# A different prologue for the attention part of a one-core attention and expert kernel: unit rows set by VectorE, idle transposes, more maxima and values before the main loop

## The reference

```python
x = x + attention(layernorm(x))      # 8 heads, each of two softmaxes over D = 32
#   q, k = x @ Wq, x @ Wkv[:, :512]; v = x @ Wkv[:, 512:]
#   w = softmax(q1 k1^T) - lam * softmax(q2 k2^T); attn = rms_norm(w @ v) * gamma
x = x + experts(layernorm(x))        # gated q, k, v projections of 16 experts,
#   causal attention with head dimension 64, gated output projections
```

## Time and profile before

| quantity | value |
|---|---|
| median of 3 runs | 1513.02 us (1511.97 to 1514.63) |
| the profiled execution | 1515.15 us, span 1513.4 us |
| first chunk of scores starts (span time) | 55.23 us |
| first maximum of the main loop starts on VectorE | 57.62 us |
| last projection of the attention part ends | about 1163.7 us |
| TensorE busy | 1398.9 us (92%) |

### The profile page before, as it was taken

The page is one execution under the profiler, slowest core; times in us unless marked ns, Lnnn a source line. Parts: engine busy times, 40 slices in busy tenths (PEclk is TensorE's granted clock), DMA queues, the critical chain, the costliest instruction groups (busy, mean ns, idle before and its releaser), DMA issues.

```text
span 1513.4 us, 56871 instructions
## 1 busy us (share of the span) xinstructions
PE 1398.9 (92%) x25690; PEld 1107.2 (73%) x25690; DVE 1022.8 (68%) x1379; ACT 854.7 (56%) x1698; POOL 554.5 (37%) x528
## 2 busy tenths in 40 slices
PE   3699999999999999999999999999996179999997
PEld 1367777777777777777777777777775169898986
DVE  5877676666766676667666676766622687888885
ACT  3255565656656555665656555565563346666663
POOL 4322323233342323243232323332232295656550
PEclk9799999999999999999999999999997579999999
DMA  4201011010101011110101011110002233333320
GB/s 117 53 14 34 15 33 25 22 36 12 45 8 39 13 34 24 24 34 13 45 6 41 13 34 24 24 34 13 3 3 44 72 144 121 147 120 129 139 93 11
DMA packets 42177, 70.34 MB, mean 46 GB/s; under 512 B 14800, under 2 KB 25296, under 8 KB 37840
## 3 DMA queue, kind: packets, MB, share of 16 engines
q1 hardware_dynamic: 40848, 65.65, 14.9%
q10 hardware_dynamic: 1088, 1.05, 0.3%
HBM read 38.88 MB, written 2.36 MB: 27 GB/s over the span
## 4 chain that ended last, share of the span: by engine, by line
PE 88%; DVE 6%; issue 2%; ACT 1%; POOL 1%; DMA 1%; ACTq 0%; SPq 0%; DVEq 0%; POOLq 0%
PE att_ps L559 31%; PE st_ps L543 15%; PE ring_ps L610 14%; PE qkv_ps L717 8%; PE ring_ps L597 4%; PE rest_ps L732 3%; DVE part_max L1181 2%; PE t_ps L805 2%; PE ring_ps L590 2%; PE ring_ps L636 2%; PE rest_ps L790 1%; PE ring_ps L628 1%; PE t_ps L757 1%; POOL z L516 1%; PE qk_ps L744 1%
## 5 line engine op out<-in xcount | busy, mean ns | idle before, releaser
L1181 DVE TENSOR_REDUCE part_max<-ring_ps 128x2 f32<-128x1024 f32 x512 | 623.8, 1223 | 328.9 <-PE ring_ps L610 319.7
L559 PEld LDWEIGHTS att_ps<-v_sb,pT 128*64 128x64 f32 x16384 | 632.8, 138 | 145.3 <-issue 28.8
L559 PE MATMUL att_ps<-v_sb,pT 128*64 128x65 f32 x16384 | 650.7, 222 | 2.4 <-issue 2.4
L872 ACT ACTIVATE pT<-st_ps 128x512 f32<-128x512 f32 x1024 | 554.5, 608 | 169.7 <-PE st_ps L543 163.4
L543 PE MATMUL st_ps<-qa,ka 98*64 98x512 f16 x2048 | 398.3, 386 | 4.4 <-issue 3.8
L610 PE MATMUL ring_ps<-ka,qa 96*64 96x512 f16 x2048 | 310.3, 382 | 9.8 <-DVE part_max L1181 5.3
L516 POOL TENSOR_TENSOR z<-xnT,rw_wide 128x512 f32<-128x512 f32 x128 | 169.5, 1331 | 108.4 <-DVE z L1372 93.4
L880 ACT ACTIVATE raw_attn<-att_ps 128x260 f32<-128x260 f32 x128 | 49.6, 388 | 205.7 <-PE att_ps L559 205.7
L543 PEld LDWEIGHTS st_ps<-qa,ka 98*64 98x64 f16 x2048 | 115.4, 110 | 67.0 <-issue 13.5
L717 PE MATMUL qkv_ps<-ew_split,z 128*128 128x192 f16 x1536 | 142.8, 252 | 11.2 <-DVE z L1372 11.2
L717 PEld LDWEIGHTS qkv_ps<-ew_split,z 128*128 128x128 f16 x1536 | 132.0, 100 | 14.5 <-issue 10.8
(11 more groups left out here) (202 smaller groups left out, 1215.1 us busy)
## 6 DMA issues: line engine op xcount, KB each, us to landing
rw_wide<-rows_of_weights SPq DMA_DIRECT2D x32, 1024.0 KB, 5.1
qa<-split SPq DMA_DIRECT2D x192, 64.0 KB, 2.0
ka<-split SPq DMA_DIRECT2D x180, 64.0 KB, 2.0
resid<-in_L_attn_x SPq DMA_DIRECT2D x4, 512.0 KB, 8.0
out<-yo SPq DMA_DIRECT2D x32, 64.0 KB, 1.5
qa<-shift_rows ACTq DMA_DIRECT2D x62, 4.0 KB
ka<-split ACTq DMA_DIRECT2D x12, 64.0 KB, 2.0
wkv_sb<-in_L_attn_Wkv SPq DMA_DIRECT2D x1, 512.0 KB, 6.1
```

What stands on the lines that cost most here:

```text
L559: mm = pe.matmul(att_ps[q0:q0 + TILE_COLS, qt * DV1:(qt + 1) * DV1], pT[:, blk % 2, kt, qt * P + q0:qt * P + q0 + TILE_COLS], v_sb[:, j % ...
L872: act.activation(pT[:, blk % 2, kt, :], st_ps[:, c % ST_BANKS, :], ACT.Exp).then_inc(exp_ok, 1)
L1181: dve.tensor_reduce(part_max[:, which % 2, 2 * quarter + m // 2, m % 2, :], pair.rearrange("p (n k) -> p n k", n=2), AX.X, ALU.max, negate ...
```

## The change

- GpSimd's two memsets of the unit rows go; VectorE does them as its first instructions, with a semaphore `units_set`.
- TensorE makes 28 transposes of the identity matrix (`WARM_UP`), whose result nobody reads, as soon as batch 0 is centred (`ln_v` 3).
- Of the 12 transfers of `ka` for step 0, SyncE issues the three of softmax 1, and ScalarE nine: three in the first half, six in the second.
- `first_values` makes the values of two steps, in eight pieces, one after each of the eight first maxima; ScalarE empties them with three activations in place of one. The entry `v` of step 1 leaves the main loop.
- The prologue's ring gets four more entries behind `shift`: two maxima of head 1 and the transposes of batches 1 and 2. They leave the main loop; the maxima of groups 0 and 1 move two slots ahead, and both shifts come earlier.
- `q` and `k` of step 2 move one block later, and so do their splits; GpSimd's splits of step 1 wait for the shifts of head 0.

```diff
+WARM_UP = 28
+FIRST_MAXIMA = [("max", 0, quarter, keys) for quarter in range(4) for keys in range(2)]
+PROLOGUE = [("ln", 0), ("q", 0), ("k", 0), ("q", 1), ("k", 1), *FIRST_MAXIMA, ("shift", 0, 0),
+            ("max", 0, 0, 2), ("ln", 1), ("max", 0, 0, 3), ("ln", 2)]
+SECOND_MAXIMA = [("max", 0, n // 2, 2 + n % 2) for n in range(2, 8)]
+MAX_AT = {
+    **dict(zip(range(6), SECOND_MAXIMA)),
+    **dict(zip([6, 7, *range(9, 23)], [("max", 1, n // 4, n % 4) for n in range(16)])),
+    **dict(zip([24, 26, 28, 30, 32, 34, 35, 36, 38, 39, 40, 42, 43, 44, 46, 47], [("max", 2, n // 4, n % 4) for n in range(16)])),
+}
+SHIFT_AT = {(1, 0): ("shift", 0, 1), (3, 1): ("shift", 1)}
...
-    if s == 7 and kb in (6, 7, 8):
-        ops.append(("ln", kb - 5))
+    if s == 7 and kb == 7:
+        ops.append(("ln", 3))
...
+        if kb in (3, 4):
+            ops.append(("qk"[kb - 3], 2))
...
 (SyncE, step 0)
+                    if j == 0 and r == 2:
+                        sp.wait_ge(ring_A, EMPTIED["A"][RING_INDEX["k", 0] + 1])
+                        sp.wait_ge(ring_V, EMPTIED["V"][RING_INDEX["k", 0] + 1])
+                        for row, part in enumerate((0, 1, 0)):
+                            sp.dma_start(ka[D * row:D * (row + 1), 0, 1, :], split[D:2 * D, 2 + part, :]).then_inc(stacked[0], 16)
 (GpSimd)
-            pool.memset(units[K_MAX:K_ALL, :], PAIR_OF_ONE).then_inc(parts_set, 1)
-            pool.memset(units[K_MAX:K_MAX + 1, :], PAIR_OF_UNIT).then_inc(parts_set, 1)
...
+            pool.wait_ge(shift_ok, 3 * shift_count(0, 0))
             split_part("q", 1)
             split_part("k", 1)
 (TensorE)
+            pe.wait_ge(c2_v, 2)
+            pe.wait_ge(ln_v, 3)
+            for n in range(WARM_UP):
+                pe.transpose(ring_ps[:, 3, 0:P], ident[:, :], ident[:, :])
+            for op in PROLOGUE:
                 ring(op)
+                if op in FIRST_MAXIMA:
+                    first_values(*divmod(FIRST_MAXIMA.index(op), 4))
 (ScalarE)
-                for r in (2 * head, 2 * head + 1):
+                for r in ((0,), (2, 3))[head]:
...
+            for half, bank in enumerate((st_ps[:, 2, :], att_ps)):
+                act.wait_ge(first_v_ps, 3 + half)
+                act.activation(v_sb[:, 1, 4 * half:4 * half + 4, :, 0:DV], bank.rearrange("p (t h d) -> p t h d", t=4, h=2),
+                               ACT.Copy).then_inc(first_v, 1)
             shift(0, 0)
+            empty(("ln", 1))
+            empty(("ln", 2))
 (VectorE)
+            dve.memset(units[K_MAX:K_ALL, :], PAIR_OF_ONE).then_inc(units_set, 1)
+            dve.wait_ge(units_set, 1)
+            dve.memset(units[K_MAX:K_MAX + 1, :], PAIR_OF_UNIT).then_inc(units_set, 1)
...
-                    if (kb, s) == (0, 7):
+                    if (kb, s) == (0, 5):
                         shifts(0, 1)
-                    if (kb, s) == (3, 0):
+                    if (kb, s) == (2, 7):
                         shifts(1)
```

More of the change, by code:

```diff
@@ L103, in ring_at @@
     if s == 7:
-        if (kb + 14) % 8 == 0 and 0 <= (kb + 14) // 8 < STEPS:
+        if kb in (3, 4):
+            ops.append(("qk"[kb - 3], 2))
+        if (kb + 14) % 8 == 0 and 3 <= (kb + 14) // 8 < STEPS:
             ops.append(("q", (kb + 14) // 8))
-        if (kb + 13) % 8 == 0 and 0 <= (kb + 13) // 8 < STEPS:
+        if (kb + 13) % 8 == 0 and 3 <= (kb + 13) // 8 < STEPS:
             ops.append(("k", (kb + 13) // 8))
-        if (kb + 4) % 8 == 0 and 0 <= (kb + 4) // 8 < STEPS:
+        if (kb + 4) % 8 == 0 and 2 <= (kb + 4) // 8 < STEPS:
             ops.append(("v", (kb + 4) // 8))
@@ L257, in block_kernel @@
         stacked, shift_in = [sem("stacked0"), sem("stacked1")], sem("shift_in")
-        first_v_ps, first_v = sem("first_v_ps"), sem("first_v")
+        first_v_ps, first_v, units_set = sem("first_v_ps"), sem("first_v"), sem("units_set")
         shift_ok = sem("shift_ok")
@@ L493, in _ @@
                     normalize((kb - 7) // 4)
+                if kb in (4, 5):
+                    split_part("qk"[kb - 4], 2)
                 for kind, lag in (("q", 13), ("k", 12)):
                     j = (kb + lag) // 8
-                    if (kb + lag) % 8 == 0 and 2 <= j < STEPS:
+                    if (kb + lag) % 8 == 0 and 3 <= j < STEPS:
                         split_part(kind, j)
@@ L537, in chunk @@
                     pe.wait_ge(shift_in, 32 * shift_count(0, 1))
-                if c < 2:
-                    pe.wait_ge(first_v, 1)
+                if c < ST_BANKS:
+                    pe.wait_ge(first_v, 2)
                 if c >= ST_BANKS:
@@ L638, in ring, with first_values @@
                 mm.then_inc(ring_ok, 1)
-            def first_values(piece):
+            def first_values(j, piece):
+                banks = (st_ps[:, 0, :], st_ps[:, 1, :]) if j == 0 else (st_ps[:, 2, :], att_ps)
                 for t in (2 * piece, 2 * piece + 1):
                     for c0 in range(0, P, TILE_COLS):
-                        mm = pe.matmul(st_ps[c0:c0 + TILE_COLS, t // 4, t % 4 * P:(t % 4 + 1) * P],
+                        mm = pe.matmul(banks[t // 4][c0:c0 + TILE_COLS, t % 4 * P:(t % 4 + 1) * P],
                                        xnT[:, t * P + c0:t * P + c0 + TILE_COLS],
-                                       wkv_sb[:, H * DV:H * DV + P], start=True, stop=True)
-                if piece == 3:
+                                       wkv_sb[:, H * DV + j * P:H * DV + (j + 1) * P], start=True, stop=True)
+                if piece % 2:
                     mm.then_inc(first_v_ps, 1)
-            for n, op in enumerate(PROLOGUE):
+            pe.wait_ge(c2_v, 2)
[3 more added lines that the diff above has]
+            for op in PROLOGUE:
                 ring(op)
-                if 6 <= n < 10:
-                    first_values(n - 6)
-            pe.wait_ge(parts_set, 3)
+                if op in FIRST_MAXIMA:
+                    first_values(*divmod(FIRST_MAXIMA.index(op), 4))
+            pe.wait_ge(units_set, 2)
             for c in range(ST_AHEAD):
@@ L944, in _ @@
                         shift((kb + 2) // 4)
-                    if (kb, s) == (1, 4):
+                    if (kb, s) == (1, 2):
                         shift(0, 1)
-                    if (kb, s) == (3, 4):
+                    if (kb, s) == (3, 3):
                         shift(1)
@@ L1254, in _ @@
             late_scales()
-            for op in PROLOGUE[5:-1]:
+            for op in FIRST_MAXIMA:
                 empty(op)
             shifts(0, 0)
-            empty(("shift", 0, 0))
+            for op in PROLOGUE[PROLOGUE.index(("shift", 0, 0)):]:
+                empty(op)
             mixing_factor()
```

8 lines of the change are left out of this document (3 added, 5 removed).

## The result

The changed kernel takes 1501.36 us (median of 4 runs, 1500.12 to 1502.0) against 1513.83 (4 runs, 1511.97 to 1515.74): ratio 0.9917, 95% interval 0.9899 to 0.9934. The forecast was 1501.9 within 1497.5 to 1507. The profiled execution has a span of 1499.5 against 1513.4, and TensorE is busy 1395.4 us, 3.5 less than in the earlier trace rows.

What follows compares the result with a forecast made beforehand. TensorE was taken to set the pace from about block 11 to the attention part's end, so savings ahead of it come through: 5.0 + 1.0 + 3.4 + 1.7 = 11.1 us, from median 1513.02 to 1501.9, range 1497.5 to 1507.

Steps and rivals of the forecast that it cites:

- start of the loop: Prologue up to the loop's first maximum: first chunk at 50.85 against 55.23, plus 0.6 of clock, together 5.0 us gained.
- two maxima fewer: Loop blocks 0 to 2: two maxima leave, 2 x (1.18 - 0.69) = 1.0 us gained.
- values of step 1, two batches' transposes: Blocks 4 to 7, bound by TensorE: values 1.7 and two batches' transposes at 0.85 leave, 3.4 us gained.
- stall of group 1's shift: Loop: shifts of group 1 now come before q2, 1.7 us gained, bounds 0 and 2.6.
- sign of being wrong: First chunk after 53, or its distance to block 12 shrinking by less than 4, would prove the prediction wrong.
- The entry: Start of the prologue: VectorE's two slow memsets take 8.8 us, batch 0 is centred at 13.3, 0.9 late.
- The clock at q0 and k0: Prologue projections: idle transposes bring q0 and k0 under 2 us each; 0.8 gained at k0's split.
- The stacking: Prologue transfers: ScalarE issues three, not six; first maximum 2.8 earlier on VectorE, TensorE can start at 33.7.
- The eight maxima: Prologue: VectorE needs 9.4 us, TensorE ends 0.6 behind; end at 45.5 against 48.24, 2.7 gained.
- The shift: Prologue, after the maxima: GpSimd waits, so three tiny VectorE instructions take 0.6 in place of 2.43.
- the rival: Prologue's gain eaten, e.g. TensorE at 1.2 GHz through all eight maxima, 4.3 over VectorE: 3 to 4 less, 1505.5; chance 0.2.
- The slower one: Rival: TensorE's clock stays low in blocks 1 and 2 too, 7 us slower, 1520; chance 0.03.

Runs made afterwards that it cites:

- e6: Changed kernel with the values of step 1 and the transposes of batches 1 and 2 back in the loop; 1505.58 us.
- e5: Changed kernel with the projections q and k of step 2, and their splits, one block earlier again, in blocks 2 and 3; 1501.94 us.
- e1: Changed kernel with the unit rows set by GpSimd again at their old place; 1500.58 us.
- e2: Changed kernel without the idle transposes (`WARM_UP = 0`); 1502.97 us.
- e10: e9 without the idle transposes (`WARM_UP = 0`); median of four runs 1498.48 us.
- e4: Changed kernel with ScalarE issuing all of the first keys again; 1503.53 us.
- e9: Changed kernel with unit rows by GpSimd in halves, mixing factor in block 3, q and k of step 2 in blocks 2 and 3; 1499.18 us, ratio 0.9905.
- e11: e9 with three idle transposes in each slot of block 0 and a wait for `first_v`; median of four runs 1499.35 us.
- e7: Changed kernel with GpSimd setting the first key buffer's unit rows early, the second's after scaling batch 3; 1498.63 us.
- e12: Kernel before, with GpSimd setting the first key buffer's unit rows early and the second's after the splits of step 1; 1513.01 us.

## Why the prediction was right

The terms, with what the marks and runs give for them:

| term | predicted | measured |
|---|---|---|
| start of the loop | 5.0 | 4.8 (block 0), 4.6 at its first maximum |
| two maxima fewer | 1.0 | 1.2 (0.8 from block 1 to block 2, 0.4 from there to block 3) |
| values of step 1, two batches' transposes | 3.4 | 4.0 (e6; 4.1 between before and e5) |
| stall of group 1's shift | 1.7, bounds 0 to 2.6 | 2.6 |
| `q` and `k` of step 2 a block later | 0 | -0.5 (e5) |
| sum | 11.1 | 12.1; block 8 comes 12.2 earlier, the attention part ends 12.4 earlier, the medians differ by 12.5 |

The stall and the first of the two maxima are read between the kernel before and e5, which has `q` of step 2 at the same place: from block 1's copy to block 2's it is 12.79 us in the one and 9.37 in the other, 3.4 less. Of this 0.8 is a maximum that before has right ahead of that projection, with a wait of 0.20 for VectorE behind it, so that the projection begins at 84.66, and that e5 has not (timeline of before):

```profile
83.86 0.60 PE L610 MATMUL ring_ps<-ka,qa 96*64 96x512 f16 x4
```

The rest, 2.6, is the stall. The mechanisms were those forecast, and neither sign of being wrong showed: the first chunk came before 53, and the distance from it to block 8, beyond which the two kernels run alike, shrank by 8.7. That the time was met to 0.5 us (1501.9 for 1501.36) is in part luck: the forecast gain of 11.1 was 1.4 too small against 12.5, and the 1513.02 that it was taken from, a median of three runs, was 0.8 below the 1513.83 that it was measured against.

**The entry.** Predicted: memsets of 8.8 us from 0.7 to 9.5, centred at 13.3. They end at 9.51, centred at 13.40. Each row reads 3.47, but the second begins 0.91 us after the first one's end, for which it waits with nothing between them, and from end to end it is 9.51 - 5.12 = 4.39, the 4.4 of the slope in the earlier trace rows. The Trainium skill's one cycle an element (VectorE: DVE Perf Modes, "Zero memsets can be issued as uint32") gives an estimate of 4.27; by the end-to-end time the trace agrees, by the row it does not. That the 0.91 belongs to the memset is inferred; no run takes the two apart. What the prediction took from one profile as a fixed cost need not be one: e1 shows the stall absent with the same two memsets. So this part of the change is a loss of 1.0 at the centring against an execution that had the stall and, as e1 beside the changed kernel has it, of 3.5 at block 8 against one that had not.

**The clock at q0 and k0.** Both in under 2 us each, as predicted; k0's split ends at 28.22 against 29.33 before, 1.1 gained for 0.8 counted. e2 gives 1.1 for the idle transposes at the first maximum and 0.3 at the loop's; e10 gives nothing.

**The stacking.** The first maximum starts 3.2 earlier on VectorE (2.8 counted), on TensorE at 33.96 (33.7 counted); e4 gives 1.9 of it to the queues.

**The eight maxima.** They cost 10.65 us against 9.4 of VectorE's own: 1.2 lost to the low clock where I had 0.6. That step was too small by half, and it took back what the start had over the forecast; they end at 45.71 (45.5 counted).

**The shift.** 0.58 in place of 2.43, as predicted. The first chunk comes 0.9 later than predicted (51.73 for 50.85), since the transposes of batch 1 ran at the low clock, 1.97 where those of batch 2 took 1.07; but from chunk to maximum it is 1.32, the 1.3 of the high clock, of which I had counted half. The mixing factor was held for 0.40 and cost nothing, as in the sum.

**The loop.** Two terms were mis-sized most. One is the transposes and values: I took a quarter microsecond off each for the overlap with the next matmul, and the marks show them at nearly their full busy time, 0.98 for each batch (blocks 6 and 8), which leaves 2.0 of e6's 4.0 for the values. The other is the stall of group 1's shift, which gave its upper bound, 2.6 for 1.7, the wait for its transfer included. I costed the move of q2 and k2 at nothing; e5 shows it at 0.5.

**The rivals.** None decided. The low clock did take something in the maxima, 1.2 of the 4.3 that the rival had. The slower one, a clock that stays low into the loop, exists in small: 1.6 to 1.8 us in four of the fourteen profiles, never in the changed kernel's own.

What stays open: what makes the spread of 2 to 4 us between executions of one kernel. The profiles show the lock at 7.6 us, the landing of batch 1, the clock and the second part at work, not their shares. The lock isn't needed for it: e9 to e11, in whose profiles it costs under 0.1 us, spread by 2.3, 3.8 and 3.2.

## What to carry to other kernels

A gain in the prologue counts only as far as the next engine, transfer or clock lets it through: follow it mark by mark to the first block at which the pacing engine runs full, and take single instructions out of that engine's full stretch at their whole slot. When a tiny instruction lasts as long as a neighbour engine's large one, look at the two start times: if they are a tenth apart, the stall may be there in some executions and not in others (here two kernels, one profile each), and the cure that worked is to make the large instruction shorter or later (e7, e12), not to hand its work to the engine that was waiting.

## What was not expected of the hardware

- The lock between GpSimd's memset and VectorE's 128x8 instruction came with a start at 7.58 and not with one at 7.49, 0.1 us of a transfer's landing: 3.60 us or 0.17.
- A VectorE memset of 4096 elements reads 3.47 us in its row and takes 4.39 from the end of the one before, on which it waits, to its own end; the missing 0.91 stands as idle time before it. All six profiles with VectorE's memsets have this pair.
- The granted clock fell at the end of the loop's block 0 to 1.2 GHz in four profiles (e2, e6, e7, e10), after a stretch in which TensorE had worked and waited for VectorE in every slot, and stayed up in the others after the same stretch; it cost 1.6 to 1.8 us.
